# State-space steps of a two-stream decoder: inputs copied by ScalarE and multiplied by GpSimd, pairs of states added by GpSimd, turns placed anew

## Chip, cores and metric

One Trainium2 chip, one core, one launch. The metric is the device time of the whole program in microseconds. Before the change it is 4295.11 us, the median of three runs (4294.72 to 4298.41).

## The reference, cut to what matters

The program is a decoder of four layers over 32 sequences of 128 tokens with 128 features. Each layer has a mixing section, a cross or second mixing section, and a feed-forward section, most of them with experts. The section that changes is the first of the last layer, a state-space layer (Mamba). For each of 256 channels and 16 states it computes, over the tokens t of a sequence,

```
state[t] = exp(delta[t] * A) * state[t-1] + (delta[t] * x[t]) * B[t]
y[t]     = sum over the 16 states of C[t] * state[t]  +  D * x[t]
```

and then y * silu(z) and an output projection. delta, B and C are projections of x, which is silu of a causal convolution of 4 taps.

## The kernel before

**Two streams in rounds.** The sequences are worked on in groups of two; a tile is 128 partitions by 256 columns (two sequences of 128 tokens). Two streams, 0 and 1, each take eight groups. In a round each stream runs all twelve sections once, but stream 0 begins with section L0_delta and stream 1 with L2_attn, so that different sections run side by side (`ROUND`, line 60). The program is a short first stretch, a loop of 7 rounds, a last stretch, and a final expert stage of its own (lines 2510 to 2606). There is a barrier behind each stretch and each round.

**The order on each engine is a table.** Every section is written as five generators, one for each engine (`pe_f`, `act_f`, `dve_f`, `pool_f`, and one for the DMA queue). Each `yield` ends a turn. `TURNS` and `LAST_TURNS` hold one string for each engine: 0 and 1 take the next turn of stream 0 or 1, and "w" in TensorE's string is a warming matmul (`warm`, line 2427; its record has line 2432): ident_bf times itself into a free bank, 128x256 in bf16, which nothing reads. All engines work strictly in their order; between engines there are semaphores. `P.open`, `P.take` and `P.give` (lines 260 to 305) hand the 8 banks of PSUM around.

**The scan loop** (`mamba`, line 1557). The 256 channels are two chunks of 128 partitions, c = 0 and 1, and the 16 states are taken in pairs, so there are 16 steps k = (c, n), n = 0, 2, ..., 14. A step works on 128x512 tiles, two states side by side, in rings of RING = 2 buffers (`decay`, `inp`, `state`, `yc`):

- TensorE spreads the rows of B and C for two states over the partitions with `sel_state` (line 1626), into one bank each (`bc1`, `bc2`).
- ScalarE computes `decay`, two exponentials of 128x256 (line 1699).
- VectorE multiplies `du` (delta times x) with the bank of B into `inp` (line 1750), runs the recurrence as one scan over 512 columns from `decay` and `inp` into `state` (line 1756), and multiplies `state` with the bank of C into `yc` (line 1762).
- TensorE adds both halves of `yc` into the bank `sum`, with two matmuls by the identity (`add_up`, line 1611); the sum of the 16 states is made in that bank.

A step's `yc` may be overwritten once the matmuls of the step two before it are done. GpSimd does little in this section: `rstd` of the norm (line 598, two columns, for both streams and all sections) and one clearing (line 1774). In other sections it has small products (lines 2273 to 2318) and clearings (lines 948, 949).

fp32 matmuls show as two records each in the profile.

## Time and profile before

| | |
|---|---|
| median of the runs | 4295.11 us |
| the profiled execution | 4291.49 us |
| its span, first to last instruction | 4289.5 us |
| mean granted TensorE clock | 0.950 of full speed |
| TensorE, VectorE, ScalarE, GpSimd busy | 92%, 72%, 46%, 15% of the span |
| matmuls, of them warming matmuls | 41486 records, 5310 |
| table loads of ScalarE | 249 on line 341, 22 on line 1273, 1 on line 1699 |

The profiled execution took 2.0 us more than its span, and 3.6 us less than the median. Busy means that at least one instruction of the engine was under way; matmuls are pipelined, and a record shows some 0.27 us for one that stands alone, though the next can follow after 0.11. PE is TensorE, DVE VectorE, ACT ScalarE, POOL GpSimd.

### The profile page before, as it was taken

Reading aid. Unit: us, or ns where it says so; the run is one execution under the profiler, and the core shown is the slowest. Engines: PE = TensorE matmul, PEld = TensorE weight load, DVE = VectorE, ACT = ScalarE, POOL = GpSimd, SP = SyncE. Lnnn points to the kernel's source line nnn. Section 1 sums busy time; section 2 is a strip of 40 time slices with the busy share of each in tenths; the row PEclk is TensorE's granted clock in tenths of the full one; section 3 lists DMA queues with packets and bytes.
Section 4 is the critical chain, followed back from the end, with each engine's and each line's share of the span. In section 5 each row is a group of like instructions: output and inputs, shape, how many; then the busy total and the mean of one; then the engine's idle time right before and its main releaser. Section 6 shows DMA issues by size and latency. Waiting matters only on the chain. (4 is left out here: it accounts for less than half of the span.)

```text
span 4289.5 us, 102291 instructions
## 1 busy us (share of the span) xinstructions
PE 3937.5 (92%) x41486; PEld 2841.4 (66%) x41486; DVE 3102.7 (72%) x8220; ACT 1977.8 (46%) x4830; POOL 654.7 (15%) x988
## 2 busy tenths in 40 slices
PE   4799999999999999999999999999999999999998
PEld 3476676766666666666676666776676666666675
DVE  4468777687876868778686886768777687875782
ACT  2254463544535444353534546345453544446551
POOL 2020201102020120211112020120202112120003
PEclk6899999999999999999999999999999999999999
DMA  6000000000000000000000000000000000000003
GB/s 165 1 2 1 9 1 9 2 1 9 1 9 2 9 2 1 10 1 9 2 9 2 1 9 2 9 2 1 9 1 9 2 8 2 2 8 1 1 1 102
DMA packets 52836, 46.15 MB, mean 11 GB/s; under 512 B 8354, under 2 KB 48914, under 8 KB 52126
## 3 DMA queue, kind: packets, MB, share of 16 engines
q1 hardware_dynamic: 48076, 33.04, 2.8%
q8 instruction: 343, 5.62, 0.5%
q0 software_dynamic: 2560, 5.79, 0.4%
q14 instruction: 143, 1.17, 0.1%
q10 hardware_dynamic: 1714, 0.54, 0.1%
HBM read 27.25 MB, written 12.62 MB: 9 GB/s over the span
## 5 line engine op out<-in xcount | busy, mean ns | idle before, releaser
L2432 PE MATMUL banks<-ident_bf 128*128 128x256 bf16 x5310 | 878.8, 278 | 37.1 <-issue 32.7
L2432 PEld LDWEIGHTS banks<-ident_bf 128*128 128x128 bf16 x5310 | 513.6, 101 | 231.9 <-issue 121.0
L883 ACT ACTIVATE scratch<-banks 128x512 f32<-128x512 f32 x512 | 279.5, 598 | 171.5 <-PE banks L807 170.6
L773 PE MATMUL banks<-scratch 32*128 32x512 f32 x2048 | 339.1, 653 | 9.9 <-DVE scratch L932 3.6
L919 DVE TENSOR_REDUCE scratch<-banks 128x4 f32<-128x512 f32 x512 | 323.2, 678 | 14.9 <-PE banks L743 5.4
L341 ACT ACT_TABLE_LOAD x249 | 319.5, 1283 | 27.6 <-PE banks L1100 23.3
L1756 DVE TENSOR_TENSOR_SCAN scratch<-scratch 128x512 f32<-128x512 f32 x256 | 312.7, 1222 | 9.1 <-ACT scratch L1699 3.2
L1699 ACT ACTIVATE scratch<-scratch,ssm_A 128x256 f32<-128x256 f32 x512 | 229.8, 503 | 164.0 <-DVE scratch L1756 162.6
L1611 PE MATMUL banks<-scratch,w_ident 128*128 128x256 f32 x1024 | 271.5, 387 | 19.6 <-DVE scratch L1762 19.6
L598 POOL TENSOR_TENSOR 0_rstd<-0_var,minus_half 128x2 f32<-128x2 f32 x96 | 74.1, 771 | 1303.3 <-DVE 0_var L616 1104.2
L1895 PE MATMUL banks<-scratch 32*32 32x32 f32 x10496 | 234.2, 206 | 33.4 <-issue 26.8
L1895 PEld LDWEIGHTS banks<-scratch 32*32 32x32 f32 x10496 | 201.3, 118 | 85.9 <-issue 62.3
L1237 PE MATMUL banks<-experts,scratch 128*128 128x128 f32 x1792 | 245.9, 283 | 7.9 <-ACT scratch L1273 4.7
L1237 PEld LDWEIGHTS banks<-experts,scratch 128*128 128x128 f32 x1792 | 230.6, 196 | 26.9 <-ACT scratch L1273 10.5
L1273 ACT ACTIVATE scratch<-banks,w_e_b 128x256 f32<-128x256 f32 x448 | 194.2, 474 | 76.4 <-PE banks L1229 70.4
L598 POOL TENSOR_TENSOR 1_rstd<-1_var,minus_half 128x2 f32<-128x2 f32 x96 | 75.1, 782 | 993.7 <-DVE 1_var L616 965.0
L823 PE MATMUL banks<-scratch 128*32 128x128 f32 x4096 | 213.6, 280 | 4.4 <-ACT scratch L883 2.6
L931 DVE RECIPROCAL scratch<-banks 128x128 f32<-128x128 f32 x128 | 122.2, 954 | 130.9 <-PE banks L823 130.0
L1611 PEld LDWEIGHTS banks<-scratch,w_ident 128*128 128x128 f32 x1024 | 177.0, 190 | 54.9 <-DVE scratch L1762 31.9
L807 PEld LDWEIGHTS banks<-scratch,sel_part_bf 128*128 128x128 bf16 x2048 | 152.3, 100 | 87.3 <-issue 21.7
L823 PE MATMUL banks<-scratch,w_slots 128*32 128x128 f32 x4096 | 206.4, 273 | 0.0
L807 PE MATMUL banks<-scratch,sel_part_bf 128*128 128x128 bf16 x2048 | 192.7, 224 | 6.5 <-ACT scratch L875 5.8
(525 smaller groups left out, 8213.9 us busy)
## 6 DMA issues: line engine op xcount, KB each, us to landing
expert_in<-scratch SPq DMA_DIRECT2D x1, 4112.0 KB, 26.6
experts<-in_e_W SPq DMA_DIRECT2D x14, 256.0 KB, 5.6
scratch<-expert_in SPq DMA_DIRECT2D x2, 1542.0 KB, 11.5
w_e_W<-in_e_W SPq DMA_DIRECT2D x3, 704.0 KB
experts<-in_e_w SPq DMA_DIRECT2D x1, 1792.0 KB, 8.7
experts<-in_e_w SPq DMA_DIRECT2D x2, 896.0 KB, 12.9
scratch<-expert_in SPq DMA_DIRECT2D x2, 514.0 KB, 4.4
0_xres<-in_x SPq DMA_DIRECT2D x8, 128.0 KB, 2.1
```

The source lines that it names most:

```text
L341: act.preload_act_table_set(name)
L773: last = pe.matmul(row_tiles(t), lhs[r, col(s)], rhs[r, s], start=True, stop=letter == "S" and mask is None, skip_group_check=True)
L807: last = pe.matmul(t[:, i * L:(i + 1) * L], sel_part[:, a:a + 1].broadcast_to([128, 128]), mT[:, col(s)], start=False, stop=i == NI - 1, s ...
L823: last = pe.matmul(t[32 * i:32 * i + 32, k * L:(k + 1) * L], W["slots"][:, 32 * j:32 * j + 32] if k else vslot[:, s, j, i, :], pT[:, s % 2 ...
L883: P.give(act.activation(pT[:, s % 2, j, :], t, ACT.Exp), f"{nm}.T{s}{j}")
L919: P.give(dve.tensor_reduce(negm[:, s, NI * j:NI * j + NI], row_tiles(t), X, ALU.max, negate=True), f"{nm}.S{s}{j}")
L1237: last = pe.matmul(t[:, col(s)], hid[:, e % RING, c, col(s)], w2[:, 2 * e + c, :], start=c == 0, stop=c == 1, skip_group_check=True)
L1611: last = pe.matmul(total[:, c * N:(c + 1) * N], ident[:], yc[:, k % RING, j, :], start=False, stop=n == DS - 2 and j == 1, skip_group_chec ...
L1699: ins = act.activation(decay[:, k % RING, j, :], dstart[:, c, :], ACT.Exp, scale=ssm_A[:, c, n + j:n + j + 1])
L1756: dve.tensor_tensor_scan(*flat, 0.0, ALU.mult, ALU.add).then_inc(ev(nm + ".state"), 1)
L1895: last = pe.matmul(t[dst, h * width:(h + 1) * width], lhs(h), rhs(h), start=True, stop=True, skip_group_check=True)
L2432: pe.matmul(banks[:, bank, 0:N].rearrange("p (s f) -> p s f", s=G), ident_bf[:], spread(ident_bf[:], G), start=True, stop=True, skip_group ...
```

## The change

In each step of the scan loop:

- ScalarE copies the bank of B to `inp` and gives the bank free; this is a turn of its own, ahead of the exponentials.
- GpSimd multiplies `inp` in place with `du`, repeated for the two states (event `.inp`). The scan waits for this event, and VectorE's multiply and its turn are gone.
- GpSimd adds the two halves of `yc` in place (`pair`, event `.pair`), one step behind its multiplies. TensorE waits for that event and adds one half of `yc` with one matmul instead of two.

All five strings of both tables are new, except those of the DMA queue. Their contents in counts:

| turns | before | after |
|---|---|---|
| warming matmuls, a round | 671 | 903 |
| warming matmuls, last stretch | 613 | 896 |
| ScalarE's turns, a round (both streams) | 470 | 502 |
| VectorE's turns, a round | 588 | 556 |
| GpSimd's turns, a round | 78 | 144 |
| table loads that follow from ScalarE's order, a round | 33 | 43 |
| table loads, last stretch | 40 | 47 |

The first stretch and the final expert stage are as before. The first lines of TensorE's string, then the functions:

```diff
 TURNS = [
-    ("w10w1wwwwwwwww00www10000w1w0wwwwwwww1wwwwwwwwwwwwwwwwwwwwwwwwwwwwwwwwwww0ww0wwwwwwwwwwwwwwwwwwwwwwwwww10w0ww"
...
+    ("00ww1wwwwwww0w10w0w00www11wwww01www1wwwwwwwww0w0wwwwwwwwww1ww1wwwwwwwwww1ww0www01wwwww00ww11ww1w0ww1w11wwww"
...
@@ -1606,10 +1612,9 @@
                             if n == 0:
                                 pe.matmul(total[:, c * N:(c + 1) * N], skip_diag[:, c, :], xc[:, c, :], start=True, stop=False,
                                           skip_group_check=True)
-                            P.wait_given(pe, f"{nm}.bc2.{c}.{n}")
-                            for j in range(2):
-                                last = pe.matmul(total[:, c * N:(c + 1) * N], ident[:], yc[:, k % RING, j, :], start=False,
-                                                 stop=n == DS - 2 and j == 1, skip_group_check=True)
+                            pe.wait_ge(ev(nm + ".pair"), k + 1)
+                            last = pe.matmul(total[:, c * N:(c + 1) * N], ident[:], yc[:, k % RING, 0, :], start=False,
+                                             stop=n == DS - 2, skip_group_check=True)
                             if k < len(steps) - 1:
                                 last.then_inc(ev(f"{u}.sum"), 1)
                             else:
@@ -1695,6 +1700,9 @@
                             tables.use(act, EXP)
                             if k >= RING:
                                 act.wait_ge(ev(nm + ".state"), k - RING + 1)
+                            t = P.take(act, f"{nm}.bc1.{c}.{n}")
+                            P.give(act.copy(inp[:, k % RING].rearrange("p j t -> p (j t)"), t), f"{nm}.bc1.{c}.{n}")
+                            yield
                             for j in range(2):
                                 ins = act.activation(decay[:, k % RING, j, :], dstart[:, c, :], ACT.Exp,
                                                      scale=ssm_A[:, c, n + j:n + j + 1])
@@ -1746,11 +1754,7 @@
                                    BIG).then_inc(ev(nm + ".start"), 1)
                         for k, (c, n) in enumerate(steps):
                             yield
-                            t = P.take(dve, f"{nm}.bc1.{c}.{n}").rearrange("p (j t) -> p j t", j=2)
-                            P.give(dve.tensor_tensor(inp[:, k % RING], spread(du[:, c, :], 2), t, ALU.mult),
-                                   f"{nm}.bc1.{c}.{n}")
-                            P.wait_given(dve, f"{nm}.bc1.{c}.{n}")
-                            yield
+                            dve.wait_ge(ev(nm + ".inp"), k + 1)
                             dve.wait_ge(ev(nm + ".decay"), k + 1)
                             flat = [r[:, k % RING].rearrange("p j t -> p (j t)") for r in (state, decay, inp)]
                             dve.tensor_tensor_scan(*flat, 0.0, ALU.mult, ALU.add).then_inc(ev(nm + ".state"), 1)
@@ -1772,6 +1776,25 @@
                         yield
                         P.wait_given(pool, nm + ".hT")
                         pool.memset(xpad[:, :, :, 0:3], 0.0).then_inc(ev(f"{u}.zero"), 1)
+
+                        def pair(k):
+                            c, n = steps[k]
+                            P.wait_given(pool, f"{nm}.bc2.{c}.{n}")
+                            pool.tensor_tensor(yc[:, k % RING, 0, :], yc[:, k % RING, 0, :], yc[:, k % RING, 1, :],
+                                               ALU.add).then_inc(ev(nm + ".pair"), 1)
+
+                        yield
+                        pool.wait_ge(ev(nm + ".start"), 1)
+                        for k, (c, n) in enumerate(steps):
+                            yield
+                            P.wait_given(pool, f"{nm}.bc1.{c}.{n}")
+                            pool.tensor_tensor(inp[:, k % RING], inp[:, k % RING], spread(du[:, c, :], 2),
+                                               ALU.mult).then_inc(ev(nm + ".inp"), 1)
+                            if k >= 1:
+                                yield
+                                pair(k - 1)
+                        yield
+                        pair(len(steps) - 1)
 
                     return pe_f, act_f, dve_f, pool_f, nothing
```

How the order moves. In these rows scratch0 and scratch1 are the working memories of streams 0 and 1, and a scan has the name SCALAR_TENSOR_TENSOR (the profile calls it TENSOR_TENSOR_SCAN). Lines of the changed kernel are some higher: its scan is line 1760, its multiply by the bank of C line 1766.

VectorE, in the round, at the start of stream 1's scan loop, before:

```order
L1756 SCALAR_TENSOR_TENSOR scratch1<-scratch1 128x512
L1762 TENSOR_TENSOR scratch1<-scratch1,banks 128x512
L1750 TENSOR_TENSOR scratch1<-scratch1,banks 128x512
L1756 SCALAR_TENSOR_TENSOR scratch1<-scratch1 128x512
L1762 TENSOR_TENSOR scratch1<-scratch1,banks 128x512
L931 RECIPROCAL scratch0<-banks 128x128
L932 TENSOR_TENSOR scratch0<-banks,scratch0 128x128
L1750 TENSOR_TENSOR scratch1<-scratch1,banks 128x512
L1756 SCALAR_TENSOR_TENSOR scratch1<-scratch1 128x512
```

and now:

```order
L1760 SCALAR_TENSOR_TENSOR scratch1<-scratch1 128x512
L1766 TENSOR_TENSOR scratch1<-scratch1,banks 128x512
L937 RECIPROCAL scratch0<-banks 128x128
L938 TENSOR_TENSOR scratch0<-banks,scratch0 128x128
L1760 SCALAR_TENSOR_TENSOR scratch1<-scratch1 128x512
L1766 TENSOR_TENSOR scratch1<-scratch1,banks 128x512
L633 TENSOR_TENSOR 0_xres<-0_xres,banks 128x256
L613 BN_STATS 0_stats<-0_xres 128x6 x2
L617 BN_AGGR 0_mv<-0_stats 128x2 x2
L622 TENSOR_SCALAR 0_var<-0_mv 128x2
```

The multiply ahead of each scan is gone, so that a scan comes right behind the last step's product by C or behind stream 0's work.

GpSimd, in the round, from stream 1's norm ahead of its scan loop, before:

```order
L598 TENSOR_TENSOR 1_rstd<-1_var,minus_half 128x2
L1774 MEMSET scratch1 128x4x3
L598 TENSOR_TENSOR 0_rstd<-0_var,minus_half 128x2 x2
L948 MEMSET scratch0 128x1024
L949 MEMSET scratch0 128x256
L598 TENSOR_TENSOR 0_rstd<-0_var,minus_half 128x2
L598 TENSOR_TENSOR 1_rstd<-1_var,minus_half 128x2
```

and now (line 1791 is the multiply, line 1783 the add of the pair):

```order
L604 TENSOR_TENSOR 1_rstd<-1_var,minus_half 128x2
L1778 MEMSET scratch1 128x4x3
L1791 TENSOR_TENSOR scratch1<-scratch1 128x512 x2
L1783 TENSOR_TENSOR scratch1<-scratch1 128x256
L1791 TENSOR_TENSOR scratch1<-scratch1 128x512
L1783 TENSOR_TENSOR scratch1<-scratch1 128x256
L604 TENSOR_TENSOR 0_rstd<-0_var,minus_half 128x2
L1791 TENSOR_TENSOR scratch1<-scratch1 128x512
L1783 TENSOR_TENSOR scratch1<-scratch1 128x256
L1791 TENSOR_TENSOR scratch1<-scratch1 128x512
```

Where GpSimd only served norms and clearings, its order now alternates multiplies and adds of stream 1, with stream 0's rstd between them.

TensorE, in the round, in stream 0's scan loop, before (line 1626 spreads B or C, line 1611 adds, line 2432 is the warming matmul):

```order
L1626 MATMUL banks<-scratch0,sel_state_bf 128x256 x2
L1611 MATMUL banks<-scratch0,w_ident 128x256 x2
L2432 MATMUL banks<-ident_bf 128x256 x4
L1626 MATMUL banks<-scratch0,sel_state_bf 128x256 x2
L2432 MATMUL banks<-ident_bf 128x256
L1626 MATMUL banks<-scratch0,sel_state_bf 128x256 x2
L2432 MATMUL banks<-ident_bf 128x256 x4
L1607 MATMUL banks<-scratch0,skip_diag 128x256
L1611 MATMUL banks<-scratch0,w_ident 128x256 x2
```

and now (lines 1631, 1616 and 2455):

```order
L1631 MATMUL banks<-scratch0,sel_state_bf 128x256 x2
L2455 MATMUL banks<-ident_bf 128x256 x6
L977 MATMUL banks<-1_hT,fw_gate 128x256
L977 MATMUL banks<-1_hT,fw_up 128x256
L2455 MATMUL banks<-ident_bf 128x256 x13
L1631 MATMUL banks<-scratch0,sel_state_bf 128x256 x2
L2455 MATMUL banks<-ident_bf 128x256 x2
L1616 MATMUL banks<-scratch0,w_ident 128x256
L2455 MATMUL banks<-ident_bf 128x256 x3
L1631 MATMUL banks<-scratch0,sel_state_bf 128x256 x2
```

There is one adding matmul in a step for two, and there are more warming matmuls between a step's parts.

## Rows read from the trace of the kernel before

**Rows 1.** The page: busy us and share of the span by engine.

```profile
PE 3937.5 (92%) x41486; PEld 2841.4 (66%) x41486; DVE 3102.7 (72%) x8220; ACT 1977.8 (46%) x4830; POOL 654.7 (15%) x988
```

**Rows 2.** Timeline of the DMA queue, stream 1's load in two rounds (start, us).

```profile
460.70 0.41 SPq L2345 DMA_DIRECT2D 1_xres<-in_x  x1
...
3534.74 0.38 SPq L2345 DMA_DIRECT2D 1_xres<-in_x  x1
```

**Rows 3.** Windows, all engines: both loops, a whole round, stream 0's last loop.

```profile
core 0: us, PE busy (x) PEld busy (x) DVE busy (x) ACT busy (x) POOL busy (x), PEclk, DMA share, GB/s
869.70:925.50 55.80, 52.99 (x484) 37.51 (x485) 52.38 (x88) 25.55 (x63) 3.43 (x4) 0.99 0.01 1
1120.70:1174.20 53.50, 52.15 (x409) 38.85 (x407) 51.11 (x85) 23.06 (x57) 3.43 (x4) 1.00 0.00 1
711.50:1223.85 512.35, 482.46 (x5151) 347.82 (x5150) 384.52 (x1023) 243.00 (x599) 78.48 (x118) 0.96 0.02 5
4122.00:4169.70 47.70, 47.12 (x350) 36.47 (x347) 46.32 (x67) 17.70 (x42) 2.07 (x3) 1.00 0.01 1
```

**Rows 4.** Windows of both loops: line 2432 on PE, then line 1750 on DVE.

```profile
869.70:925.50 55.80, 12.72 (x72) 6.65 (x69) 0.99 0.01 1
1120.70:1174.20 53.50, 21.51 (x128) 11.92 (x125) 1.00 0.00 1
...
869.70:925.50 55.80, 10.20 (x15) 0.99 0.01 1
1120.70:1174.20 53.50, 10.19 (x15) 1.00 0.00 1
```

**Rows 5.** Groups by line: xcount, busy us, mean ns of one, idle before.

```profile
L1756 DVE TENSOR_TENSOR_SCAN scratch<-scratch 128x512 f32<-128x512 f32 x256 | 312.7, 1222 | 9.1 <-ACT scratch L1699 3.2
L1762 DVE TENSOR_TENSOR scratch<-scratch,banks 128x512 f32<-128x512 f32 x256 | 175.4, 685 | 6.9
L1750 DVE TENSOR_TENSOR scratch<-scratch,banks 128x512 f32<-128x512 f32 x256 | 174.1, 680 | 12.6 <-PE banks L1626 11.3
L883 ACT ACTIVATE scratch<-banks 128x512 f32<-128x512 f32 x512 | 279.5, 598 | 171.5 <-PE banks L807 170.6
L341 ACT ACT_TABLE_LOAD x249 | 319.5, 1283 | 27.6 <-PE banks L1100 23.3
L2313 POOL TENSOR_TENSOR scratch<-scratch 128x512 f32<-128x512 f32 x32 | 33.7, 1074 | 434.8 <-DVE scratch L2231 434.8
L2301 POOL TENSOR_TENSOR scratch<-scratch 128x256 f32<-128x256 f32 x32 | 19.6, 611 | 0.0
```

**Rows 6.** Timeline of PE in the loops: runs of matmuls (start, us, xcount).

```profile
888.67 1.03 PE L1611 MATMUL banks<-scratch,w_ident 128*128 128x256 f32 x4
...
4150.23 0.60 PE L1607 MATMUL banks<-scratch,skip_diag 128*128 128x256 f32 x2
...
885.64 0.60 PE L2432 MATMUL banks<-ident_bf 128*128 128x256 bf16 x4
...
889.54 0.49 PE L2432 MATMUL banks<-ident_bf 128*128 128x256 bf16 x3
```

**Rows 7.** GpSimd beside VectorE: timelines, line 2273's durations (ns), means of line 924, 925.

```profile
25.79 3.46 POOL L2273 TENSOR_TENSOR scratch<-scratch 128x256 f32<-128x256 f32 x1 [7.08 <-ACT scratch L2012]
...
25.90 0.35 DVE L2107 TENSOR_SCALAR scratch<-scratch,w_d_local_w 128x256 f32<-128x256 f32 x1
...
28.27 0.48 DVE L2104 SCALAR_TENSOR_TENSOR scratch<-scratch,w_d_mid_w 128x256 f32<-128x256 f32 x1
...
L2273 POOL TENSOR_TENSOR scratch<-scratch x16: 653/693/3458, 25.8 to 3805.7; 128x256 f32<-128x256 f32 x16
...
510.45 1.71 POOL L2284 TENSOR_TENSOR scratch<-scratch,w_blocks 128x128 f32<-128x128 f32 x4
...
511.06 0.31 DVE L924 TENSOR_TENSOR scratch<-scratch 128x16 f32<-128x16 f32 x1
511.40 0.38 DVE L925 CAST scratch<-scratch 128x16 bf16<-128x16 f32 x1
...
L925 DVE CAST scratch<-scratch 128x16 bf16<-128x16 f32 x128 | 23.9, 187 | 4.4
L924 DVE TENSOR_TENSOR scratch<-scratch 128x16 f32<-128x16 f32 x128 | 25.1, 196 | 4.4
...
1095.15 1.26 DVE L621 TENSOR_SCALAR 0_hn<-0_xres,0_mv,0_rstd 128x128 f32<-128x128 f32 x2 [0.81 <-POOL 0_rstd L598]
```

**Rows 8.** Windows, all engines (columns of rows 3): a slow clock, the round's end.

```profile
791.50:807.50 16.00, 15.55 (x146) 13.26 (x136) 8.90 (x32) 3.20 (x12) 0.69 (x1) 0.68 0.00 1
...
1111.50:1223.85 112.35, 110.02 (x975) 80.54 (x973) 92.03 (x218) 49.31 (x110) 10.72 (x14) 1.00 0.03 8
```

More of the change, by code:

```diff
@@ L92 @@
+    ("01001100000001011100000011111111011111111001111011111111111111101100110111101011101011101011110100000001100"
+     "0000001001000000000000000000111001000"),
     ("111000"),
@@ L117 @@
+    ("01100100000010010000011000000011001101011111010111110110111111111111010111110011001000000000000000000000000"
+     "1000000000100"),
     ("110010"),
```

97 lines of the change are left out of this document (49 added, 48 removed).

## The prediction

> **What bounds the kernel now.** I read the page first, for the busy shares: TensorE 92%, VectorE 72%, ScalarE 46%, GpSimd 15% [rows 1]. A share of the whole says little here, because two streams run different layers at the same time. The chain of waits covers only the last section of the kernel, which isn't changed. So I looked up how long a round is (stream 1's load is issued at 460.70 and, six rounds later, at 3534.74: 512.3 us a round [rows 2]) and then asked for the busy time of every engine in the stretches where a scan loop runs [rows 3]. From the first scan of a loop to its 16th, stream 1 takes 55.8 us and stream 0 53.5 us. VectorE is busy for 52.4 and 51.1 of them: it is the bound there, and both loops together are 109 of the round's 512 us. In the last stretch, stream 0's loop takes 47.7 us with VectorE at 46.3. TensorE shows 53.0 and 52.2, but 12.7 and 21.5 us of that are warming matmuls [rows 4], which compute nothing. ScalarE (25.6, 23.1) and GpSimd (3.4, 3.4) have room.
>
> Outside the loops the round isn't bound by VectorE. In the whole round it is busy for 384.5 us, TensorE for 482.5, so 29.9 us of TensorE's row are free [rows 3].
>
> **The change part by part.**
> 1. VectorE loses the multiply of line 1750: 15 of them are 10.2 us of either loop [rows 4], 0.680 us each [rows 5], 256 x 0.680 = 174 us in all. In the loops nearly all of that is on the path now.
> 2. TensorE loses one of two adding matmuls a step. Four records of line 1611 in a row take 1.03 us, two take 0.60, so each further record is 0.215 us and a dropped matmul (two records) 0.43: 32 a round, 13.8 us. This isn't on the path while VectorE is the bound.
> 3. TensorE gets 232 more warming matmuls a round (903 for 671) and 283 more in the last stretch. Four in a row take 0.60 us, three 0.49 [rows 6]: 0.108 each. That is 25.1 us a round; with item 2, TensorE's fixed work grows by 11.3 us a round and 16.7 in the last stretch. The cover is its 29.9 idle us. Gone, the price is the whole.
> 4. ScalarE gets one 128x512 copy out of a bank a step; the nearest row, an activation of that size from a bank, is 0.598 us [rows 5]: 16 x 0.6 = 9.6 us a loop. Its order also has 43 table loads a round instead of 33, and 47 for 40 in the last stretch, at 1.283 us: 12.8 more. With that, ScalarE has 45 and 40 us of work in the loops, its order priced with these rows: below VectorE, but no longer far below.
> 5. GpSimd gets a 128x512 multiply with a repeated operand and a 128x256 add per step. The nearest rows are 1.074 us (line 2313, the same size, also with a repeated operand) and 0.612 (line 2301): 1.69 a step, 27 us a loop, 54 a round. From above, a 128x256 product on GpSimd has taken 3.46 us [rows 7]; below the nearest rows I see no reason for a gain.
> 6. The scan now waits for a chain: banks, ScalarE copy, GpSimd multiply, then the scan. What is queued behind it on VectorE is the other stream's work.
>
> **What items 5 and 6 cost.** The trace shows VectorE and GpSimd getting in each other's way. Line 2273's product starts at 25.79, while VectorE runs products of two scratch operands (line 2104) and scalings of one (line 2107) back to back until 28.75, and it takes 3.46 us; its median is 0.69 [rows 7]. The other way round, VectorE's small product of line 924 takes 0.31 us and the cast of line 925 0.38 under GpSimd products, where their means are 0.196 and 0.187 [rows 7]. Operations of VectorE that read a bank don't show it: the product of line 1762 keeps 0.685. The scan reads two scratch operands, so I count it among those that exclude GpSimd. Then a step holds both for 1.222 + 1.074 + 0.612 = 2.91 us, and no step is shorter, however little other work VectorE has. In the new order, VectorE's instructions from one scan to the next, priced with these rows, come to 1.9 to 6.8 us a step and to 47.1 and 45.8 us a loop. With every step under 2.91 raised to 2.91, they are 51.3 and 50.8. I add about 0.1 us a step for handing over and take 52.5 and 52: 3.3 and 1.5 us less than now, of the 9 or so that VectorE's order has shed.
>
> The Trainium skill (SBUF — State Buffer, Who interferes with whom) says that a Vector instruction with two SBUF inputs and a GpSimd instruction that reads SBUF exclude each other for their whole length, and that one with at most one SBUF input doesn't contend. By that rule, the trace agrees for lines 2273 and 924; no run here shows it for the scan. By the rule the sum is 4279 us; if the scan and GpSimd never met, it would be the first rival's 4177.
>
> **Sum.** Loops -4.8 us a round. For the rest of the round I take +2: 11.3 us more of fixed TensorE work, most in places where it idles, against some clock regained, since the round's granted clock is 0.96 and drops to 0.68 in the worst 16 us [rows 8]. That is -2.8 x 7 = -19.6. In the last stretch, stream 0's loop goes from 47.7 to about 46, but behind it TensorE is 47.1 of 47.7 us busy [rows 3] and gets more warming matmuls there: +5. So +3.3. Together -16.3 us: from the profiled 4291.5 (span 4289.5 and 2.0 around it) to 4275.2. The median of the runs lies 3.6 above the profiled execution, so **4279**. A difference of 0.2% (8.6 us) is about what a measurement can tell from none.
>
> **Rivals.**
> - *VectorE's relief comes through whole.* GpSimd's operations fall beside VectorE's reads from banks (0.685 of the multiply and about 1.2 of the other stream's work a step), and the loops follow VectorE's and TensorE's own work: about 48.5 us each, -12.3 a round. The added warming matmuls hold the clock where it falls: -4. Then -16.3 x 7 - 4 = -118: 4177. For it: VectorE's saturation. Against: the new order is uneven, with steps of 1.9 us in which nothing covers GpSimd. Chance 0.22.
> - *Scans wait on GpSimd (slower).* GpSimd's multiply for the next step is ready shortly before this step's scan, starts first, and the scan waits for half of 1.07 us on average. That gives 0.54 us a step back, or 8 us a loop, and the loops are where they were. Besides, in GpSimd's order the other stream's rstd now stands behind operations of the loop which wait; now it is served at once (0.81 us before line 621 in the worst case seen [rows 7]). With two norms in a loop, 2 us each, and the ten table loads, a round gets 7 us longer: 4295.1 + 49 + 5 = 4349. It decides from 0.3 us a step on. Chance 0.25.
> - *TensorE becomes the bound (slower).* Its 29.9 idle us are latency which warming matmuls can't replace, so the added work is paid in full: 11.3 x 7 + 16.7 = +96: 4391. For it: 110.0 of 112.4 us busy at the round's end [rows 8]. Against: VectorE is as full there. Chance 0.13.
>
> **How the numbers follow.** The forecast has 0.40, with a range of its own of 4250 to 4305: 0.24 faster, 0.12 the same, 0.04 slower. Faster is 0.22 + 0.24 = 0.46, the same 0.12, slower 0.25 + 0.13 + 0.04 = 0.42. The range of 8 in 10 takes in both middle rivals and leaves out the far half of the first and most of the last: 4180 to 4370.
>
> **What would show it.** Right: the loops at 52 to 53 us; VectorE's idle time in them up from 3 us to 6 or more, with GpSimd as the releaser or with scans longer than 1.22 us; GpSimd's multiply longer than 1.07 us on average. Scans that keep 1.22 us and loops of 48 speak for the first rival; loops of 55, with waits of line 621 on rstd, for the second; TensorE without gaps and rounds of 524 us for the third. The forecast is wrong if GpSimd's multiply is far from 1.07 us when undisturbed, or if most of the difference lies outside the loops.

## The result, and the profile after

The changed kernel takes 4534.9 us (median of four runs, 4530.98 to 4540.87) beside 4296.8 for the kernel before: ratio 1.0559, 95% interval 1.0546 to 1.0571. The forecast was 4279, its range ended at 4370. So the result is 238 us slower where a small gain was forecast, on the side of the second and third rival but far beyond both.

The page of the profile, as in [rows 1]:

```profile
span 4528.8 us, 105887 instructions
PE 4027.3 (89%) x42881; PEld 2869.7 (63%) x42881; DVE 3065.3 (68%) x7964; ACT 2204.5 (49%) x5163; POOL 1179.4 (26%) x1500
```

VectorE and TensorE fill a smaller share of the span than before; the time is waiting. Stream 1's load, as in [rows 2]:

```profile
480.04 0.41 SPq L2368 DMA_DIRECT2D 1_xres<-in_x  x1
...
3722.73 0.38 SPq L2368 DMA_DIRECT2D 1_xres<-in_x  x1
```

Six rounds are 3242.7 us, so a round is 540.4 instead of 512.3: +28.1. The 239.3 us of the span are 19.3 up to the first load (stream 1's first loop lies there), 6 x 28.1 = 168.6, and 51.3 behind the last load. The windows as in [rows 3], for a stream 1 loop, a stream 0 loop, about a round, and stream 0's last loop:

```profile
core 0: us, PE busy (x) PEld busy (x) DVE busy (x) ACT busy (x) POOL busy (x), PEclk, DMA share, GB/s
1986.50:2056.50 70.00, 58.90 (x499) 39.00 (x500) 50.01 (x75) 39.43 (x81) 34.19 (x34) 0.90 0.00 1
2253.30:2316.90 63.60, 53.40 (x480) 37.19 (x482) 51.38 (x73) 34.92 (x78) 34.31 (x34) 1.00 0.00 1
1986.50:2525.70 539.20, 490.43 (x5321) 348.49 (x5323) 379.77 (x990) 271.99 (x642) 142.93 (x182) 0.98 0.02 5
4349.40:4407.80 58.40, 49.21 (x363) 35.25 (x362) 44.50 (x56) 23.98 (x55) 34.09 (x34) 0.96 0.00 1
```

The loops have gone from 55.8 and 53.5 us to about 70 and 64, and VectorE, which had filled 94 and 96% of them, now fills 71 and 81%. Between the loops next to nothing changed: from the last scan of one loop to the first of the next it was 195.5 and 208.0 us (mean over the rounds) and is 197.4 and 208.9. The groups by line, as in [rows 5], and the waits (us in total, times, longest) say who is late:

```profile
L1760 DVE TENSOR_TENSOR_SCAN scratch<-scratch 128x512 f32<-128x512 f32 x256 | 372.8, 1456 | 194.3 <-POOL scratch L1791 165.7 <-ACT scratch L1707 27.6
L1766 DVE TENSOR_TENSOR scratch<-scratch,banks 128x512 f32<-128x512 f32 x256 | 175.4, 685 | 10.1 <-PE banks L1631 2.7
L1791 POOL TENSOR_TENSOR scratch<-scratch 128x512 f32<-128x512 f32 x256 | 327.2, 1279 | 823.5 <-ACT scratch L1704 821.5
L1783 POOL TENSOR_TENSOR scratch<-scratch 128x256 f32<-128x256 f32 x256 | 202.2, 790 | 88.6 <-DVE scratch L1766 88.6
L1704 ACT COPY scratch<-banks 128x512 f32<-128x512 f32 x256 | 150.4, 587 | 352.6 <-PE banks L1631 334.1 <-DVE scratch L1760 16.1
```
```profile
ACT scratch L1704 <- PE banks L1631: 334.1, 163, 5.3
DVE scratch L1760 <- POOL scratch L1791: 165.7, 88, 3.6
PEld banks L1616 <- POOL scratch L1783: 150.8, 154, 2.2
```

Followed backwards: the scan waits for GpSimd's multiply (1791), that for ScalarE's copy (1704), that for TensorE's spreading matmuls (1631); and in TensorE's order the adding matmul (1616), which waits for GpSimd's pair add (1783), stands in front of the next spreading. The pair add stands behind the multiply on GpSimd. That is a closed cycle: from multiply to pair add, adding, spreading, copy and the next multiply. Here it is turning, near the end of a loop (start, us):

```profile
2051.35 1.28 POOL L1791 TENSOR_TENSOR scratch<-scratch 128x512 f32<-128x512 f32 x1 [1.74 <-ACT scratch L1704]
...
2052.59 0.74 POOL L1783 TENSOR_TENSOR scratch<-scratch 128x256 f32<-128x256 f32 x1
2052.67 1.73 DVE L1760 TENSOR_TENSOR_SCAN scratch<-scratch 128x512 f32<-128x512 f32 x1 [1.26 <-POOL scratch L1791]
2053.38 0.30 PEld L1616 LDWEIGHTS banks<-scratch,w_ident 128*128 128x128 f32 x2 [0.40 <-POOL scratch L1783]
...
2054.02 0.38 PE L1631 MATMUL banks<-scratch,sel_state_bf 96*128 96x256 bf16 x2
...
2054.50 0.59 ACT L1704 COPY scratch<-banks 128x512 f32<-128x512 f32 x1 [1.44 <-PE banks L1631]
...
2055.16 1.27 POOL L1791 TENSOR_TENSOR scratch<-scratch 128x512 f32<-128x512 f32 x1 [1.84 <-ACT scratch L1704]
```

From multiply to multiply it is 3.81 us: 1.24 to the pair add's start, 0.79 to the adding matmul, 0.64 to the spreading, 0.48 to the copy, 0.66 to the multiply. The forecast's floor for a step was 2.91. Such a step needs 1.9 us of VectorE (1.22 and 0.685).

How often is it like this? In the 14 loops of the rounds there are 196 steps from a loop's second multiply on. None takes less than 3.68 us from multiply to multiply, so the cycle is a floor. In 79 of them each link follows the last with hardly a gap (at most 0.6 us between adding and spreading, 0.25 elsewhere), and these take 3.85 us on average. The mean of all 196 is 4.68: in the other 117 something more stands in a link, such as a turn of the other stream. So the cycle is a part of what makes 70 and 64 us, and not all of it.

The same rows show a lock between VectorE and GpSimd. Sorted by what GpSimd was doing, the 256 scans of the changed kernel give (worked out from all starts and durations):

| GpSimd, and the scan's start | scans | mean us |
|---|---|---|
| no operation beside the scan | 74 | 1.216 |
| an operation that starts later than the scan | 45 | 1.219 |
| a pair add under way, 0.59 to 0.66 us of it left | 91 | 1.727 |
| a pair add under way, less than 0.2 us of it left | 17 | 1.214 |
| a multiply under way, 1.2 us of it left | 14 | 2.287 |
| a multiply under way, 0.05 us of it left | 7 | 1.210 |
| a clearing or another section's product under way | 8 | 1.212 |

Whichever starts first keeps its length and the other waits. 15 pair adds that began 0.16 us behind a scan took 1.575 us for 0.725, and those scans kept 1.216. All 256 scans took 60 us more than before. That settles what no run had shown for the scan: it and a GpSimd operation that reads exclude each other. By the rule of the Trainium skill (SBUF — State Buffer, Who interferes with whom), that a two-input Vector instruction meets GpSimd's reads and not its writes, filling a buffer with a constant should cost a scan nothing. The trace of run e16 agrees: 24 fills by GpSimd lay wholly inside scans, and both kept their lengths (0.524 and 0.311 us, 1.215 to 1.226).

The prediction gave that rule's other half without its exception. The Trainium skill (SBUF — State Buffer, Who interferes with whom) says that a Vector instruction with at most one SBUF input doesn't contend with GpSimd only outside the 2-port modes. The prediction's own row of the cast of line 925 (0.38 us for 0.187) didn't fit without it. Nor do the scalings of line 627, which read one tile: alone they take 0.342 us, beside a GpSimd multiply and pair add 1.26 (18 of them), and beside two clearings, which only write, 1.09 (16). Whether they run in such a mode no run here shows.

### The profile page after: what moved, and what is told of

Same layout as the page of the kernel before. It is cut to its first block and busy times, and to the rows that moved or that the text cites. A ratio compares the mean times of both kernels' runs of the same rounds, so it can differ in the third digit from the quotient of the medians.

```text
span 4528.8 us, 105887 instructions
## 1 busy us (share of the span) xinstructions
PE 4027.3 (89%) x42881; PEld 2869.7 (63%) x42881; DVE 3065.3 (68%) x7964; ACT 2204.5 (49%) x5163; POOL 1179.4 (26%) x1500
## 5 line engine op out<-in xcount | busy, mean ns | idle before, releaser
L2455 PE MATMUL banks<-ident_bf 128*128 128x256 bf16 x7217 | 1155.4, 277 | 59.0 <-issue 37.4
L2455 PEld LDWEIGHTS banks<-ident_bf 128*128 128x128 bf16 x7217 | 694.1, 101 | 292.5 <-issue 126.8
L1791 POOL TENSOR_TENSOR scratch<-scratch 128x512 f32<-128x512 f32 x256 | 327.2, 1279 | 823.5 <-ACT scratch L1704 821.5
L1760 DVE TENSOR_TENSOR_SCAN scratch<-scratch 128x512 f32<-128x512 f32 x256 | 372.8, 1456 | 194.3 <-POOL scratch L1791 165.7
L925 DVE TENSOR_REDUCE scratch<-banks 128x4 f32<-128x512 f32 x512 | 321.9, 679 | 25.6 <-PE banks L752 12.8
L1704 ACT COPY scratch<-banks 128x512 f32<-128x512 f32 x256 | 150.4, 587 | 352.6 <-PE banks L1631 334.1
L779 PE MATMUL banks<-scratch 32*128 32x512 f32 x2048 | 307.5, 651 | 13.0 <-DVE scratch L916 10.9
L1616 PE MATMUL banks<-scratch,w_ident 128*128 128x256 f32 x512 | 180.6, 436 | 104.3 <-POOL scratch L1783 101.0
L1918 PE MATMUL banks<-scratch 32*32 32x32 f32 x10496 | 224.3, 201 | 19.1 <-issue 12.3
L1918 PEld LDWEIGHTS banks<-scratch 32*32 32x32 f32 x10496 | 190.0, 114 | 76.1 <-issue 55.9
L1783 POOL TENSOR_TENSOR scratch<-scratch 128x256 f32<-128x256 f32 x256 | 202.2, 790 | 88.6 <-DVE scratch L1766 88.6
```

The source lines that it names most:

```text
L779: last = pe.matmul(row_tiles(t), lhs[r, col(s)], rhs[r, s], start=True, stop=letter == "S" and mask is None, skip_group_check=True)
L925: P.give(dve.tensor_reduce(negm[:, s, NI * j:NI * j + NI], row_tiles(t), X, ALU.max, negate=True), f"{nm}.S{s}{j}")
L1760: dve.tensor_tensor_scan(*flat, 0.0, ALU.mult, ALU.add).then_inc(ev(nm + ".state"), 1)
L1783: pool.tensor_tensor(yc[:, k % RING, 0, :], yc[:, k % RING, 0, :], yc[:, k % RING, 1, :], ALU.add).then_inc(ev(nm + ".pair"), 1)
L1791: pool.tensor_tensor(inp[:, k % RING], inp[:, k % RING], spread(du[:, c, :], 2), ALU.mult).then_inc(ev(nm + ".inp"), 1)
L1918: last = pe.matmul(t[dst, h * width:(h + 1) * width], lhs(h), rhs(h), start=True, stop=True, skip_group_check=True)
```

## The experiments

First theory: the new work costs what the loops lost. Rivals: the new turns cost it, or the warming matmuls do. The loops' lengths below are means over the rounds, stream 1's and stream 0's; a round is from one stream 1 loop's first scan to the next. The kernel before was timed anew beside each group of runs, with medians from 4296 to 4306 us, so differences between groups are safer by the ratios.

| run | us | ratio to before, interval | loops | round | table loads |
|---|---|---|---|---|---|
| before | 4296 to 4306 | 1 | 55.6, 53.5 | 512.7 | 277 |
| changed | 4534.9 | 1.0559 (1.0546, 1.0571) | 70.3, 64.0 | 540.5 | 354 |
| e1 | 4515.4 | 1.0521 (1.0504, 1.0539) | 71.9, 63.5 | 539.3 | 354 |
| e2 | 4491.4 | 1.0461 (1.0443, 1.0478) | 68.4, 61.1 | 534.0 | 354 |
| e3 | 4514.2 | 1.0516 (1.0499, 1.0534) | 72.1, 62.2 | 538.5 | 354 |
| e8_fewer_warm | 4602.1 | 1.0715 (1.0697, 1.0733) | 70.4, 65.2 | 550.0 | 354 |
| e4 | 4879.2 | 1.1350 (1.1323, 1.1377) | 88.6, 76.7 | 581.7 | 280 |
| e6 | 4529.1 | 1.0529 (1.0503, 1.0554) | 68.9, 64.5 | 540.0 | 346 |
| e5 | 4680.3 | 1.0878 (1.0850, 1.0905) | 81.0, 70.5 | 557.9 | 354 |
| e7 | 4510.2 | 1.0479 (1.0454, 1.0505) | 70.0, 63.2 | 538.6 | 346 |
| e8_silus_together | 4511.6 | 1.0486 (1.0456, 1.0516) | 69.6, 63.4 | 537.9 | 319 |
| e9 | 4413.0 | 1.0253 (1.0225, 1.0280) | 56.7, 57.0 | 526.7 | 277 |
| e10 | 4565.6 | 1.0601 (1.0568, 1.0633) | 65.9, 64.7 | 545.4 | 283 |
| e11 | 4440.8 | 1.0319 (1.0290, 1.0348) | 61.5, 59.3 | 527.9 | 331 |
| e12 | 4451.9 | 1.0349 (1.0325, 1.0373) | 63.3, 60.9 | 529.0 | 354 |
| e13 | 4456.3 | 1.0356 (1.0335, 1.0376) | 60.4, 59.6 | 531.8 | 277 |
| e14 | 4578.1 | 1.0640 (1.0617, 1.0663) | 72.4, 63.2 | 544.6 | 331 |
| e15 | 4440.8 | 1.0318 (1.0295, 1.0342) | 61.4, 59.3 | 527.8 | 289 |
| e16 | 4372.1 | 1.0167 (1.0145, 1.0189) | 60.7, 54.2 | 519.5 | 354 |
| e17 | 4530.2 | 1.0542 (1.0524, 1.0559) | 69.2, 63.4 | 539.4 | 354 |

**Which part?** e1 puts VectorE's multiply back (into the scan's turn) and undoes the pair add; e2 undoes the pair add alone, e3 the inputs' part alone. All keep the new turns. Where an order would block with other work, a few entries are exchanged: in e1, e3, e5, e7, e8_silus_together and e12 in the last part, in e4, e10 and e13 in the round, and e10's last part goes by the new turns.

```diff
-                            dve.wait_ge(ev(nm + ".inp"), k + 1)
+                            t = P.take(dve, f"{nm}.bc1.{c}.{n}").rearrange("p (j t) -> p j t", j=2)
+                            P.give(dve.tensor_tensor(inp[:, k % RING], spread(du[:, c, :], 2), t, ALU.mult),
+                                   f"{nm}.bc1.{c}.{n}")
+                            P.wait_given(dve, f"{nm}.bc1.{c}.{n}")
...
-                            pe.wait_ge(ev(nm + ".pair"), k + 1)
-                            last = pe.matmul(total[:, c * N:(c + 1) * N], ident[:], yc[:, k % RING, 0, :], start=False,
+                            P.wait_given(pe, f"{nm}.bc2.{c}.{n}")
+                            for j in range(2):
+                                last = pe.matmul(total[:, c * N:(c + 1) * N], ident[:], yc[:, k % RING, j, :], start=False,
```

> The work of before (VectorE multiplies out of the bank, TensorE adds both states), placed by the new turns. Theory A (the new work costs: copy, GpSimd multiply and pair add stand in every scan's chain, 24.3 us of the 28.1 us a round lie in the two loops): 4290 to 4340 us, loops 54 to 60 us each, round 512 to 520. Rival B (the new turns cost, whatever work they place): 4480 us or more, loops above 62 us. Rival C (the 232 further warming matmuls a round bound TensorE): 4380 to 4420 us with the loss spread over the round and not in the loops.

> The changed kernel with the pair add undone: GpSimd only multiplies, TensorE adds both states itself as before. Theory A1 (TensorE waits for the pair add in front of the next spreading matmuls, so the pair add lies in the loop's chain: 0.73 us on GpSimd and its hand-overs, some 1 us a step in 32 steps a round): 16 to 32 us a round less, 4320 to 4430 us. Rival A2 (copy, table loads and multiply alone make the step's length): within 30 us of 4535. By the scans' waits for an add under way (90 scans of 1.688 us against 1.216 without) alone: 0.47 x 90 = 42 us less, of which what is on the path, 4495 or more.

> The changed kernel with the inputs' part undone: VectorE multiplies out of the bank as before, GpSimd adds the pair, the turns are the new ones. Theory A1 (the pair add's wait on TensorE is what lengthens the loop): 4430 us or more. Rival A2 (copy, table loads and GpSimd multiply make the step's length): 4290 to 4360 us, with ScalarE's table loads back near 280 from 354.

> The changed kernel with 232 warming matmuls a round and 283 in the last taken out evenly, so that their number is that of before; order of all else as in the changed kernel. Theory A (the loops are bound by a chain over four engines): within 25 us of 4535. Rival C (TensorE bound by the further matmuls, 0.109 us each, 25 us a round): 4380 us or less. If they hold the clock up: slower than 4535, with the granted clock under 0.961.

e8_fewer_warm deletes 232 letters "w" of TensorE's round (903 to 671) and 283 of the last part. The first theory fell: with none of the new work the new turns still take 4515 us (e12 below corrects this to 4452). So did the plain rival C: fewer warming matmuls made the kernel 67 us slower, 8.7 us a round of it in the gap in front of stream 1's loop (217.6 us for 208.9), and its mean granted clock went from 0.961 to 0.934. e2 lies between the ranges that were expected: without the pair add the kernel is 1.0% faster, no more. TensorE's adding matmuls wait for the product by C there and no longer for GpSimd, but ScalarE and VectorE wait nearly as long as before:

```profile
ACT scratch L1705 <- PE banks L1632: 296.1, 176, 5.8
DVE scratch L1761 <- POOL scratch L1790: 167.0, 90, 3.5
```

So the pair add's link isn't what holds most of the steps. e3 came out in its first theory's range, but it has e1's late multiply, so the pair add can't be judged by it.

**Turns or tables?** e4 is the new work in the order of before (copy and exponentials in one turn). e6 moves one line, e7 does the same in e1. e5 moves the spreading of step k+1's inputs ahead of the adding matmul.

```diff
                             yield
-                            tables.use(act, EXP)
                             if k >= RING:
...
                             yield
+                            tables.use(act, EXP)
                             for j in range(2):
```

> The new work (copy by ScalarE, multiply and pair add by GpSimd, one adding matmul) placed by the turns of before: TensorE's, ScalarE's and VectorE's orders of before with the copy set in front of the exponentials of its step, GpSimd's order that of the change, and a few turns exchanged where they would block each other. The old work under the new turns took 4515 us of the 4535. Theory B (the placement costs, the work hardly anything): 4260 to 4350 us, loops 53 to 60 us. Theory D (the new turns were fitted to the new work, and each cost is covered by the other): above 4400 us, loops above 60. The forecast's own sum for the work alone: 4279.

> The changed kernel with ScalarE's choice of the exponential table moved behind the copy, to the turn of the exponentials themselves, so that a turn of the other stream between the two no longer makes the table go and come back. Theory T (the 77 further table loads of 1.283 us lie in the steps' chain, some 8 a round): 8 x 1.28 = 10 us a round less, 4430 to 4470 us, table loads near 280. Rival (they lie in ScalarE's idle time, 49% busy): within 15 us of 4535.

> The changed kernel with TensorE's spreading matmuls of step k+1's inputs set in front of the adding matmul of step k-1 instead of behind it, which takes TensorE's adding out of the cycle copy, multiply, pair add, add, spreading, copy. If that cycle holds the loops: 64 to 75 us become 56 to 62, 4380 to 4450 us. If the order of the other stream's work between the steps holds them, as the run with the old work under the new turns suggests: within 30 us of 4535.

> The old work under the new turns, as in the run of 4515 us, with the exponential table chosen in the turn of the exponentials. If the table loads are what the new turns cost: 4290 to 4400 us, with table loads near 280 instead of 354. If it is the order of the turns otherwise: 4480 us or more, even with fewer loads.

The new work in the old turns is worst of all, so the new turns do their part for it. In e4 the scans wait 367 us for GpSimd's multiply and TensorE 318 for the pair add, as in the cycle above, and the mean granted clock is 0.898:

```profile
DVE scratch L1756 <- POOL scratch L1787: 367.1, 180, 7.5
PEld banks L1612 <- POOL scratch L1779: 318.2, 155, 4.7
```

e6 and e7 took out only 8 of 77 loads, since most come from the other stream's gating activations between two steps, and gained about 5 us each by the medians, 0.3 and 0.4% by the ratios, which the intervals hardly tell from nothing. e5 was a miss: it cuts one link of the cycle, but is 145 us slower. TensorE's wait for the pair add did fall (45.5 us), but scans now wait for the exponentials (98.2 us) as well:

```profile
DVE scratch L1764 <- POOL scratch L1795: 146.3, 64, 6.6
DVE scratch L1764 <- ACT scratch L1711: 98.2, 37, 6.3
PEld banks L1616 <- POOL scratch L1787: 45.5, 52, 3.1
PEld banks L2459 <- DVE scratch L1770: 160.9, 56, 5.0
```

The last line is a new wait: TensorE's warming matmuls, which take a free bank, wait 160.9 us for VectorE's product by C to give one back, where it was 16.2 us in the changed kernel. The early spreading opens a bank sooner, so the wait for the pair add was traded for one for banks. How much of the 145 us this is, and why the exponentials came late, stays open.

**Single causes.** e8_silus_together exchanges six entries of ScalarE's order in e1. e9 adds 232 and 283 letters "w" to the kernel before. e10 and e11 have the inputs' part alone with ScalarE's two turns of a step changed about, e10 in the turns of before, e11 in the new ones:

```diff
-                            t = P.take(act, f"{nm}.bc1.{c}.{n}")
-                            P.give(act.copy(inp[:, k % RING].rearrange("p j t -> p (j t)"), t), f"{nm}.bc1.{c}.{n}")
-                            yield
                             for j in range(2):
                                 ins = act.activation(decay[:, k % RING, j, :], dstart[:, c, :], ACT.Exp,
                                                      scale=ssm_A[:, c, n + j:n + j + 1])
                             ins.then_inc(ev(nm + ".decay"), 1)
+                            yield
+                            t = P.take(act, f"{nm}.bc1.{c}.{n}")
+                            P.give(act.copy(inp[:, k % RING].rearrange("p j t -> p (j t)"), t), f"{nm}.bc1.{c}.{n}")
```

> The old work under the new turns (4515 us), with six entries of ScalarE's order of a round exchanged, so that the two gating activations of the other stream's network stand together in front of a step's exponentials instead of one in front and one behind. Table switches by the order of a round: 33, where the new turns have 38 and the turns of before 31. Theory O (the new order's placement in the loops costs: VectorE waits 3.5 us once a loop for the second gating activation behind two table loads): 5 x 1.28 + 3.5 = 6 to 10 us a round less, 4435 to 4475 us. Rival (ScalarE's order does not matter, the loop waits elsewhere): within 15 us of 4515.

> The kernel before with 232 warming matmuls a round and 283 in the last added, each behind one that was there, all else in its old order. It tells what their number costs by itself. If TensorE, 95% busy in the loops of before, takes each as 0.109 us on the path (rival C): up to 25 us a round, 4400 to 4490 us, which would be most of the new turns' cost. If they fill its idle time: within 30 us of 4296, and faster where they raise the granted clock of 0.950.

> Only the inputs' part of the change (copy by ScalarE, multiply by GpSimd), under the turns of before for the rounds (the last part goes by the new turns); the copy stands behind the exponentials of its step instead of in front, so that its wait for TensorE no longer holds them up. Theory W (the copy in front of the exponentials takes their lead over the scan, 4 us in the kernel before, 0.6 to 1 after): rounds of 495 to 520 us, loops 48 to 58, 4240 to 4400 us with the last part slower by 60. Rival D (any order not fitted to the new work is bad, as with the 4879 us): above 4600.

> Inputs only under the new turns (4491 us), with ScalarE's two turns of a step changed about: exponentials, then the copy. Theory W (exponentials behind the copy wait for TensorE's spreading, and the scan with them): 4400 to 4470 us. Rival (the scan waits for copy and multiply, which now come one exponential pair, 1.0 us, later): 4500 to 4600 us.

e9: the warming matmuls alone cost the kernel before 2.5%, 14 us a round, 0.06 us each. Of that, 9.4 us lie between the loops. Its granted clock stayed (0.951 for 0.950), so they bought nothing. e8_silus_together: 35 table loads fewer than e1, and 4 us (0.35% by the ratios, whose intervals overlap); table loads are a small part at most. e11 shows that, with the inputs alone, the copy's place costs. Over stream 1's loop the exponentials had ended 4.3 us (median) before their scan began in the kernel before; in the changed kernel and in e2 it is 0.6, since the copy's wait for TensorE stands in front of them; in e11 it is 3.7, and the run is 50 us faster than e2 (1.4% by the ratios). e10 misses its range: with the order of before in the rounds this work is slower than with the new one. But e4, e10 and e13 also have 232 warming matmuls fewer a round than the new turns and lower granted clocks (0.898, 0.931 and 0.928, e11 0.973). No run has the old order with this work and more warming matmuls, so order and clock aren't told apart there.

**What is left.** e12 is e1 with VectorE's multiply of step k+1 right behind step k's product by C. e13 is the kernel before plus the pair add. e14 is the whole change with exponentials first, e15 is e11 with the six exchanged entries of e8_silus_together.

```diff
                             P.give(dve.tensor_tensor(yc[:, k % RING], state[:, k % RING], t, ALU.mult),
                                    f"{nm}.bc2.{c}.{n}")
+                            if k + 1 < len(steps):
+                                multiply(k + 1)
```

> The old work under the new turns once more, but VectorE multiplies step k+1's inputs right behind step k's product by C, as the kernel before does in most steps, and no longer in the scan's own turn. If the 4515 us were an artefact of that place (the multiply late, its bank held, TensorE waiting 3.35 us for it once): 4380 to 4440 us, loops 57 to 62, that is before plus the warming matmuls. If the new orders cost by themselves: 4480 or more, loops above 62.

> The kernel before with the pair add alone moved to GpSimd and one adding matmul a step; its own orders but for a few exchanged entries, GpSimd's with the pair turns of the change. If TensorE, 95% busy in the loops, sets their end and the pair add is in time (forecast, item 2: 13.8 us a round less): 4180 to 4240 us. If TensorE now waits for the pair add in the order it has, with its 0.73 us and hand-overs: 4310 to 4500 us; the scans wait for adds under way, 0.47 us each, at most 128 + 112 us in all.

> The whole change with ScalarE's two turns of a step changed about: the exponentials, then the copy. With the inputs alone that took 4491 to 4441 us. If the copy's wait for TensorE in front of the exponentials is what the whole change loses too: 4460 to 4500 us, the lead of the exponentials over the scan back above 2 us, and fewer table loads (331 there). If the pair add's wait on TensorE rules instead: within 20 us of 4535.

> Inputs only, exponentials before the copy (4441 us), and the other stream's two gating activations together, as in the run e8, where it was worth 4 us. If table loads are hidden: 4425 to 4445. If they come onto the path once the copy no longer does: 4390 to 4420.

e12 corrects e1: 64 us of its 4515 (1.7% by the ratios) were my own construction, the late multiply that held its bank; e3, e7 and e8_silus_together have it too. e12's time lies between the two ranges that were expected. What stays is 1.0349, still 1% above e9, and it speaks against the forecast's way of reckoning. VectorE's work is that of before, and the loops are 7.7 and 7.4 us longer than before, 6.6 and 3.9 longer than in e9:

```profile
core 0: us, PE busy (x) PEld busy (x) DVE busy (x) ACT busy (x) POOL busy (x), PEclk, DMA share, GB/s
1947.20:2010.50 63.30, 57.20 (x529) 41.08 (x530) 53.23 (x90) 31.13 (x66) 4.22 (x4) 1.00 0.01 2
2205.70:2266.60 60.90, 57.94 (x497) 43.27 (x495) 51.91 (x87) 27.92 (x64) 4.22 (x4) 1.00 0.00 1
```

e13: the pair add alone costs the old order 3.6%. Its loops' windows show TensorE relieved (50.1 for 53.0 us), waiting, and at a lower clock (mean of the run 0.928 for 0.950):

```profile
1963.40:2023.00 59.60, 50.12 (x460) 33.67 (x462) 53.15 (x87) 25.09 (x62) 14.38 (x19) 0.93 0.00 1
2223.70:2283.50 59.80, 50.85 (x379) 35.60 (x377) 52.50 (x86) 23.26 (x58) 14.44 (x19) 0.94 0.00 1
```

e14 fell outside both of its ranges: exponentials first made the inputs alone 50 us faster and the whole change 43 slower. The exponentials have their lead again (4.4 us), but the waits inside the cycle grew, TensorE's for the pair add from 150.8 to 189.7 and the scan's for the multiply from 165.7 to 220.2:

```profile
DVE scratch L1760 <- POOL scratch L1791: 220.2, 113, 4.0
PEld banks L1616 <- POOL scratch L1783: 189.7, 176, 3.2
```

This fits a cycle into which the copy comes later; that the copy's place is the link wasn't shown by itself. e15 gained nothing over e11, with 42 table loads fewer.

**GpSimd's length, and the warming matmuls in the loops.**

```diff
-                            pool.tensor_tensor(inp[:, k % RING], inp[:, k % RING], spread(du[:, c, :], 2),
-                                               ALU.mult).then_inc(ev(nm + ".inp"), 1)
+                            pool.memset(inp[:, k % RING], 0.01).then_inc(ev(nm + ".inp"), 1)
...
-                            pool.tensor_tensor(yc[:, k % RING, 0, :], yc[:, k % RING, 0, :], yc[:, k % RING, 1, :],
-                                               ALU.add).then_inc(ev(nm + ".pair"), 1)
+                            pool.memset(yc[:, k % RING, 0, :], 0.01).then_inc(ev(nm + ".pair"), 1)
```

> The whole change with GpSimd's multiply and pair add each replaced by filling the same output with a constant: same order, waits and signals, but GpSimd reads nothing. Left out are the product of the inputs with delta u and the sum of the two states. If scans wait for GpSimd's reads (1.688 us where a pair add was under way at their start, 1.216 alone), the mean of the 256 scans falls from 1.456 to 1.22, 60 us in all. If these 60 us are on the path: 4440 to 4490 us, less still where the fill is much shorter than the 1.27 and 0.73 us it replaces (its length is read from the run). If the loops are held by the cycle through TensorE: the scans get shorter and the time stays above 4500 as long as the fills last about as long.

> The whole change with 67 of the 303 warming matmuls a round that stand among the steps of the two scans taken out (49 in stream 1's, 18 in stream 0's), which brings the number in the loops to that of the kernel before; those between the loops and in the last part stay. If they hold the loops up: 67 x 0.109 = up to 7 us a round, 4480 to 4510 us, with the clock in the loops where it was. If the loops wait for the chain over ScalarE and GpSimd: within 15 us of 4535. If the clock falls in the loops: slower than 4550.

e16's groups, and below them TensorE's wait for the pair:

```profile
L1790 POOL MEMSET scratch<- 128x512 f32 x256 | 134.2, 524 | 909.2 <-ACT scratch L1704 909.1
L1783 POOL MEMSET scratch<- 128x256 f32 x256 | 79.6, 311 | 119.2 <-DVE scratch L1766 119.1
L1760 DVE TENSOR_TENSOR_SCAN scratch<-scratch 128x512 f32<-128x512 f32 x256 | 312.6, 1221 | 154.6 <-ACT scratch L1707 154.6
```
```profile
PEld banks L1616 <- POOL scratch L1783: 25.6, 40, 1.0
```

With every wait in its place, but the two operations 0.76 and 0.48 us shorter and the scans back at 1.221, the kernel is 163 us faster (3.9 of the 5.6% by the ratios). TensorE's wait for the pair falls from 150.8 to 25.6 us, and the scan no longer waits for GpSimd but, 154.6 us, for the exponentials behind the copy. Of the 196 steps only 7 are left in which each link of the cycle follows at once, and these take 2.49 us. GpSimd's length and the lock together are thus worth most of the 238 us in this order; the run doesn't part them, since a fill is shorter too. e17 gained 5 us, within the runs' scatter: in the changed kernel the warming matmuls among the steps aren't what holds the loops.

No run was faster than the kernel before, so no better version is put forward.

## Why the prediction was wrong

**The step that failed is in "What items 5 and 6 cost":** "Then a step holds both for 1.222 + 1.074 + 0.612 = 2.91 us, and no step is shorter", with every shorter step raised to 2.91 and "about 0.1 us a step for handing over". That takes a loop to be as long as VectorE's order, priced, or the lock of two engines, whichever is longer. The lock is real. But the least length of a step is that of a cycle through three in-order engines, GpSimd, TensorE and ScalarE: at least 3.68 us and 3.81 in the rows above, with three hand-overs and the adding and spreading matmuls in it. Item 6 named half of it (banks, copy, multiply, scan) and looked at what is queued behind the scan; it didn't ask what stands behind the pair add's new wait on TensorE, namely the spreading that feeds the next copy, nor behind the copy's on ScalarE, namely the exponentials. The loops came out at 70 and 64 for 52.5 and 52.

The loops at 1986.50 and 2253.30 show what this floor was worth by the forecast's own reckoning. With VectorE's work from scan to scan as it was, each scan taken as 1.222 us, and every shorter step raised to 2.91, they come to 53.4 and 53.9 us; raised to 3.68, to 60.3 and 59.6. This estimate puts some 6 to 7 us a loop down to the floor. The other 10 and 4 us aren't explained by any floor under VectorE's order. They are waits in steps that are longer than the cycle, and e12, which has no such cycle, has loops of 63 and 61 as well. They weren't followed one by one.

The forecast's floor of 2.91 wasn't one either: stream 1's loops have a step in which the scans start 1.85 us apart. A stretch from one scan to the next needn't hold both of GpSimd's operations.

**The premise was too weak as well.** "VectorE is the bound there" was true of one order: a VectorE 94% busy says that the others keep ahead of it in that order, not that they will in another. e12 has VectorE's old work and loops of 63 and 61.

**By item.** 1: VectorE lost 174 us of work as priced, but its busy time fell by 37, since 60 came back in the scans, 37 in the scalings of line 627 (189.3 us for 152.2), which meet GpSimd too, and the rest in other small operations, 11 of it in line 916. 2: a matmul less a step didn't help: with the pair add alone (e13) the kernel is 3.6% slower at a lower clock. 3: the rest of the round was forecast at +2 us and came to +2.8 between the loops. In the old order the same number of warming matmuls costs 14 us a round (e9), of 25.1 priced. 4: copy 0.587 for 0.6 us, 77 more table loads, both as counted; the loads cost little (e15), but the item had no price for the copy's place in front of the exponentials, 1.4% with the inputs alone (e11). 5: GpSimd's two operations took 1.279 and 0.790 us for 1.074 and 0.612. Undisturbed they take 1.274 and 0.725, so the nearest rows were 0.20 and 0.11 too short, and 0.06 of the add is the lock. By e16, where 1.23 us less of GpSimd and 0.24 of the scan a step give 0.64 us a step back (163 / 256), I estimate 0.43 us per us, some 42 us for the mis-sizing of 0.38 us in 256 steps. The last stretch, forecast +3.3, lost 51.3, some 40 of it in its own two loops (122.6 us for 93.4, stream 1's, and 58.3 for 47.0).

**The rivals.** "Scans wait on GpSimd" had the right sign and place, its lock (0.23 us a scan instead of 0.54) and its wait; it missed the way back through TensorE. "TensorE becomes the bound" isn't borne out for the changed kernel: e17 gains nothing clear and e8_fewer_warm is slower, though at a lower clock. In the old order the warming matmuls alone do cost 2.5% (e9), so its price was real there.

**How the 238 us add up.** By the ratios along one chain of kernels: before to e9 (warming matmuls) 2.5%; to e12 (the rest of the new turns) 1.0%; to e2 (inputs) 1.1%; to the change (pair add) 1.0%. So by this chain 3.5 of the 5.6% come with the new turns and 2.1 with the new work. The intervals are about 0.3% either way, and the shares depend on the way taken: the pair add is worth -0.05% from e1 to e3 (both with the late multiply), 1.0% from e2 to the change, 3.2% from e11 to e14 and 3.6% in the old order. So it is a cost of the combination, not a sum of prices. What in the new turns, besides the warming matmuls, makes the old work's loops 6.6 and 3.9 us longer stays open; table loads are a small part of it at most.

## What to carry to other kernels

When a step moves to another engine, write its chain down as a ring over the engines' orders, through what stands behind each new wait, and add durations and hand-overs all the way round. A step can't be shorter than that, however idle the busiest engine is; it can be longer, by whatever else stands in a link. Do it above all where the result comes back to an engine that also feeds the start of the chain. A saturated engine in the profile is the bound only of the order it was measured in, so price a moved step with the old work under the new order too.

## What the runs showed of the hardware

A scan of two scratch operands that starts under a GpSimd operation which reads waits for most of what is left of it: 0.51 of 0.65 us under the pair add, 1.07 of 1.21 under the multiply, next to nothing where 0.18 or less is left. A fill on GpSimd costs it nothing (24 wholly inside scans), and a VectorE product with one operand from a bank (line 1766) kept 0.685 us on average (0.672 to 0.689 over all 256). A scaling of a single scratch operand (line 627, 0.34 us alone) took 1.26 where it met a GpSimd multiply and add, and 1.09 beside two clearings. A 128x512 multiply in place took 1.274 us on GpSimd against 0.524 for filling as much. And more warming matmuls can be pure cost (e9, clock 0.951 for 0.950), while taking out as many elsewhere lowered the clock (e8_fewer_warm, 0.934 for 0.961) and cost 1.5%.
